# A fused RWKV, latent-attention and mixture-of-experts block: both high halves of the keys go into the stack by DMA, and the normalisations and the values' eviction go from VectorE to ScalarE

## The reference, cut to what matters

```python
x = x + rwkv(_layernorm(x))           # k, r projections; a scan over time; sigmoid(r) * y; Wo
x = x + ffn(_layernorm(x)), where ffn(x) is:
h   = _rmsnorm(x, gamma1)
q   = h @ Wq + bq                                  # [b, t, 16, 32]
k,v = split(((h @ Wdown + bdown) @ Wup + bup))     # through a latent of 64
att = softmax(einsum('bthd,btgd->bthg', q, k) / sqrt(32))   # over the 16 heads of ONE token
x   = x + (att applied to v) @ Wo + bo
h2  = _rmsnorm(x, gamma2)
out = x + sum over 8 experts of gate_e * (h2 @ We[e])       # all experts, softmax gate
```

## Time and profile before

| | us |
|---|---|
| runs | 3332.51, 3334.51, 3334.67 (median 3334.51) |
| the profiled execution, own time | 3332.17 |
| its span | 3330.30 |
| mean granted TensorE clock | 0.941 of full speed |

### The profile page before, as it was taken

The page is one execution under the profiler, slowest core; times in us unless marked ns, Lnnn a source line. Parts: engine busy times, 40 slices in busy tenths (PEclk is TensorE's granted clock), DMA queues, the critical chain, the costliest instruction groups (busy, mean ns, idle before and its releaser), DMA issues.

```text
span 3330.3 us, 53600 instructions
## 1 busy us (share of the span) xinstructions
PE 2887.2 (87%) x18864; PEld 1791.2 (54%) x18864; DVE 2476.6 (74%) x4548; ACT 956.6 (29%) x1823; POOL 686.1 (21%) x745
## 2 busy tenths in 40 slices
PE   2359999998888989989998898999889998999889
PEld 2235555554555655555564555555555555555544
DVE  5797777778777768777777777768777777877753
ACT  2243232322332322322331332232233232232320
POOL 0111222212122212222221222221222221212210
PEclk9669999999999999999999999999999999999999
DMA  6011111101111101111111111111111110111110
GB/s 192 15 24 20 33 33 26 30 24 33 20 33 27 33 20 33 20 33 26 33 27 26 20 33 30 29 26 27 27 26 33 27 33 20 32 21 33 26 20 13
DMA packets 588333, 102.96 MB, mean 31 GB/s; under 512 B 556562, under 2 KB 556690, under 8 KB 588050
## 3 DMA queue, kind: packets, MB, share of 16 engines
q1 hardware_dynamic: 588068, 99.40, 16.4%
HBM read 48.49 MB, written 16.78 MB: 20 GB/s over the span
## 4 chain that ended last, share of the span: by engine, by line
PE 62%; DVE 23%; issue 7%; SPq 5%; DMA 2%; ACT 0%; POOL 0%; DVEq 0%; ACTq 0%; POOLq 0%
PE bank L1049 49%; PE bank L1201 6%; DVE mcol L954 4%; SPq L424 4%; DVE zz L865 3%; PE bank L1079 3%; DVE ks L943 3%; DVE wkv L839 2%; PE bank L1191 2%; DMA qs<-m 2%; DVE acc L1028 1%; DVE wkv L827 1%; PE bank L1165 1%; DVE ht L935 1%; DVE zz L832 1%
## 5 line engine op out<-in xcount | busy, mean ns | idle before, releaser
L1049 PE MATMUL bank<-w_e,h2t 128*128 128x512 f16 x6144 | 1479.4, 398 | 19.1 <-DVE acc L1028 19.1
L1049 PEld LDWEIGHTS bank<-w_e,h2t 128*128 128x128 f16 x6144 | 617.9, 103 | 757.5 <-issue 123.1
L1028 DVE SCALAR_TENSOR_TENSOR acc<-bank,gates,acc 128x512 f32<-128x512 f32 x512 | 373.6, 737 | 164.7 <-PE bank L1049 163.6
L1201 PEld LDWEIGHTS bank<-vp,pr 128*128 128x128 f32 x2048 | 263.9, 197 | 24.0 <-DVE hrow L970 3.9
L1201 PE MATMUL bank<-vp,pr 128*128 128x33 f32 x2048 | 259.7, 275 | 3.8 <-ACT pr L608 2.7
L608 ACT ACTIVATE pr<-bank,col 128x512 f32<-128x512 f32 x256 | 171.9, 685 | 316.1 <-PE bank L1191 315.7
L865 DVE RECIPROCAL zz<-zz 128x256 f32<-128x256 f32 x128 | 219.1, 1733 | 46.8 <-POOL zz L462 46.8
L1049 PE MATMUL bank<-w_o,xo 128*128 128x512 f16 x768 | 174.3, 384 | 58.8 <-DVE xo L799 58.8
L455 POOL TENSOR_TENSOR e<-wkv 128x512 f32<-128x512 f32 x64 | 72.1, 1127 | 645.6 <-DVE wkv L827 645.6
L1191 PE MATMUL bank<-qs,ks 106*128 106x128 f16 x1024 | 104.5, 236 | 113.9 <-DMA qs<-m 113.9
L1182 PE MATMUL bank<-ks,qs 104*128 104x128 f16 x1024 | 90.8, 231 | 125.7 <-DMA ks<-k 65.7
(11 more groups left out here) (177 smaller groups left out, 3918.1 us busy)
## 6 DMA issues: line engine op xcount, KB each, us to landing
qs<-qo SPq DMA_DIRECT2D x384, 64.0 KB, 3.0
xk<-in_attn_x SPq DMA_DIRECT2D x32, 512.0 KB, 3.9
x<-in_attn_x SPq DMA_DIRECT2D x32, 512.0 KB, 3.6
result<-acc SPq DMA_DIRECT2D x32, 512.0 KB, 2.8
ks<-k SPq DMA_DIRECT2D x128, 64.0 KB, 3.0
w_e<-in_ffn_We SPq DMA_DIRECT2D x7, 1024.0 KB, 13.8
qs<-m SPq DMA_DIRECT2D x256, 2.0 KB, 1.7
qs<-in_attn_Wk SPq DMA_DIRECT2D x1, 1024.0 KB, 5.5
```

The costliest lines, as they stand in the source:

```text
L1028: V.scalar_tensor_tensor(out=acc[:, s, :], in0=moe_bank[u % 2][:, :], scalar=gates[:, s, e:e + 1], in1=acc[:, s, :], op0=ALU.mult, op1=ALU ...
L1049: ins = nc.tensor.matmul(dst, left(a), right(b), start=(n == 0), stop=(n == last))
L1201: ins = nc.tensor.matmul(att_bank[ATT_BANK["PV", k]][:, n * (HD + 1):(n + 1) * (HD + 1)], pr[:, k % 2, n * P:(n + 1) * P], vp[:, 4 * k + n ...
```

## The change

The first block of k high and the second are sent by SP like q's: with first = (0, 2) SP issues 8 DMAs for k high after ACT's last high half of k, and then the 4 for k low. DVE's copies and the piece att_stack are gone. ACT evicts the values. The normalisations become ACT instructions scale * x + bias, with bias = -mean * rstd, which DVE forms in one small instruction ("shift"; two in att_norm). att_norm2 is an ACT copy with a scale. att_rest moves in ORDER to behind att_vt, on ACT and on POOL.

```diff
 ORDER = [
...
-    ("moe", 1), ("att_turn", 0), ("att_rest", 0), ("mix_k", 0), ("att_latent", 0), ("att_q", 0),
-    ("att_up", 0), ("mix_v", 0), ("mix_decay", 0), ("att_stack", 0), ("moe", 2), ("mix_exp", 0),
-    ("mix_sum", 0), ("att_vt", 0), ("moe", 3), ("mix_rec", 0), ("mix_rec", 1), ("mix_scan", 0), ("moe", 4),
+    ("moe", 1), ("att_turn", 0), ("mix_k", 0), ("att_latent", 0), ("att_q", 0),
+    ("att_up", 0), ("mix_v", 0), ("mix_decay", 0), ("moe", 2), ("mix_exp", 0),
+    ("mix_sum", 0), ("att_vt", 0), ("att_rest", 0), ("moe", 3), ("mix_rec", 0), ("mix_rec", 1), ("mix_scan", 0), ("moe", 4),
...
-        stack_in = Steps(sem("stack_in"), 16, qk=16)
+        stack_in = Steps(sem("stack_in"), 16, qk=24)
...
             def att_up(t, _):
-                for src, dst, name, first in ((qo16, qs, "q", (0, 1)), (k16, ks, "k", ())):
-                    rest = 2 if first else 1
+                for src, dst, name, first in ((qo16, qs, "q", (0, 1)), (k16, ks, "k", (0, 2))):
+                    rest = 3 - sum(first)
...
+            def pre_norm(t, _):
+                act.wait_ge(*pre_dve.done(t, "shift"))
+                for s in range(SUB):
+                    nc.scalar.activation(xk_rows[:, s, :], xk_rows[:, s, :], ACT.Identity, bias=nb1[:, s:s + 1], scale=rs1[:, s:s + 1])\
+                        .then_inc(pre_act.sem, 1)
...
+            def att_norm(t, _):
+                act.wait_ge(*att_dve.done(t, "shift"))
+                if t.back(1):
+                    act.wait_ge(*att_pe.done(t.back(1), "T21"))
+                for s in range(SUB):
+                    nc.scalar.activation(h_rows[:, s, :], x1[t.par][:, s, :], ACT.Identity, bias=nb2[:, 1, s:s + 1], scale=rs2[:, 1, s:s + 1])\
+                        .then_inc(att_act.sem, 1)
+
+            def att_rest(t, _):
+                if t.back(1):
+                    act.wait_ge(*acc_pool.done(t.back(1), "acc"))
+                for s in range(SUB):
+                    nc.scalar.activation(x2[:, s, :], x1[t.par][:, s, :], ACT.Identity, bias=nb2[:, 0, s:s + 1], scale=rs2[:, 0, s:s + 1])\
+                        .then_inc(att_act.sem, 1)
...
             def att_up(t, _):
                 heads(t, "K", "k", k16, colof["kk"], bks, "k_lo", "q_lo")
+                if t.back(1):
+                    act.wait_ge(*att_dve.done(t.back(1), "ot_lo"))
+                for b in range(CB):
+                    act.wait_ge(*att_pe.done(t, f"V{b // 2}"))
+                    nc.scalar.activation(va32[:, :, b, :], att_bank[ATT_BANK["V", b // 2]][:, (b % 2) * T:(b % 2) * T + T]
+                                         .rearrange("p (g j) -> p g j", g=G), ACT.Identity, bias=bvcol[:, b:b + 1], scale=colof["vv"])\
+                        .then_inc(att_act.sem, 1)
...
+            def att_norm2(t, _):
+                act.wait_ge(*att_pool.done(t, "rms"))
+                for s in range(SUB):
+                    nc.scalar.activation(h_rows[:, s, :], x2[:, s, :], ACT.Copy, scale=rs3[:, s:s + 1]).then_inc(att_act.sem, 1)
...
             def att_norm(t, _):
-                xa = x1[t.par]
                 dve.wait_ge(*att_pool.done(t, "rstd"))
-                for s in range(SUB):
-                    V.tensor_scalar(h_rows[:, s, :], xa[:, s, :], mv2[:, s, 0:1], rs2[:, 1, s:s + 1],
-                                    ALU.subtract, ALU.mult).then_inc(att_dve.sem, 1)
...
+                for n in range(2):
+                    V.scalar_tensor_tensor(out=nb2[:, n, :], in0=mv2[:, :, 0], scalar=-1.0, in1=rs2[:, n, :], op0=ALU.mult, op1=ALU.mult)\
+                        .then_inc(att_dve.sem, 1)
...
-            def att_stack(t, _):
-
-                dve.wait_ge(*att_act.done(t, "k"))
-                for f in range(4):
-                    for n in (0, 2):
-                        V.tensor_copy(ks[n * HD:(n + 1) * HD, :, f, :],
-                                      grouped(k16, 0)[f * HD:(f + 1) * HD].rearrange("p g b j -> p g (b j)")).then_inc(att_dve.sem, 1)
...
             def att_max(t, n):
                 if n == 0:
                     pe.wait_ge(*stack_in.done(t, "qk"))
-                    pe.wait_ge(*att_dve.done(t, "stack"))
```

More of the change, by code:

```diff
@@ L280, in build @@
         wkv_pool = ("d1", 1), ("d2", 1), ("den", 1)
-        pre_dve = Steps(sem("pre_dve"), stats=2, idle=1, aggr=2, norm=2)
+        pre_dve = Steps(sem("pre_dve"), stats=2, idle=1, aggr=2, shift=1)
+        pre_act = Steps(sem("pre_act"), norm=2)
         pre_pool = Steps(sem("pre_pool"), eps=1, rstd=1)
@@ L286, in build @@
         att_pe = Steps(sem("att_pe"), **{f"{n}{k}": 1 for n, k in ATT_USES})
-        att_act = Steps(sem("att_act"), h_hi=2, c=2, q=8, k=8, ex=8, ot_hi=2, sq=2,
-                        h2_hi=2)
-        att_dve = Steps(sem("att_dve"), stats=2, idle=1, aggr=2, var=2, h=2, h_lo=2, xn=2, c_lo=1, v=4, stack=8,
-                        vt=1, smax=8, m_turn=1, m_hi=1, m_lo=1, norm=16, ot=1, ot_lo=2, x2=2, h2=2, h2_lo=2)
+        att_act = Steps(sem("att_act"), h=2, h_hi=2, c=2, q=8, k=8, v=4, xn=2, ex=8, ot_hi=2, sq=2,
+                        h2=2, h2_hi=2)
+        att_dve = Steps(sem("att_dve"), stats=2, idle=1, aggr=2, var=2, shift=2, h_lo=2, c_lo=1,
+                        vt=1, smax=8, m_turn=1, m_hi=1, m_lo=1, norm=16, ot=1, ot_lo=2, x2=2, h2_lo=2)
         gate_dve = Steps(sem("gate_dve"), gl=1, gmax=1, gsub=1, gsum=1, grec=1, gmul=1, gates=1)
         gate_act = Steps(sem("gate_act"), ge=1)
-        att_pool = Steps(sem("att_pool"), rstd=1, xb=2, q_lo=4, k_lo=4, rms=2)
+        att_pool = Steps(sem("att_pool"), rstd=1, q_lo=4, k_lo=4, xb=2, rms=2)
         acc_pool = Steps(sem("acc_pool"), acc=2)
@@ L635, in moe_gate @@
                 nc.scalar.activation(gl[:, :, :], gl[:, :, :], ACT.Exp).then_inc(gate_act.sem, 1)
-            pipeline(act, {"mix_turn": mix_turn, "mix_k": mix_k, "mix_v": mix_v, "mix_exp": mix_exp,
+            pipeline(act, {"pre_norm": pre_norm, "att_norm": att_norm, "att_rest": att_rest, "att_norm2": att_norm2, "mix_turn": mix_turn, "mix_k": mix_k, "mix_v": mix_v, "mix_exp": mix_exp,
                            "mix_num": mix_num, "mix_split": mix_split, "att_turn": att_turn,
@@ L811, in pre_norm @@
                 dve.wait_ge(*pre_pool.done(t, "rstd"))
[L812 to L814 removed]
+                V.scalar_tensor_tensor(out=nb1[:, :], in0=mv1[:, :, 0], scalar=-1.0, in1=rs1[:, :], op0=ALU.mult, op1=ALU.mult)\
+                    .then_inc(pre_dve.sem, 1)
             def mix_turn(t, _):
@@ L906, in att_norm @@
             def att_norm(t, _):
-                xa = x1[t.par]
                 dve.wait_ge(*att_pool.done(t, "rstd"))
-                for s in range(SUB):
-                    V.tensor_scalar(h_rows[:, s, :], xa[:, s, :], mv2[:, s, 0:1], rs2[:, 1, s:s + 1],
-                                    ALU.subtract, ALU.mult).then_inc(att_dve.sem, 1)
-            def att_rest(t, _):
-                xa = x1[t.par]
-                if t.back(1):
-                    dve.wait_ge(*acc_pool.done(t.back(1), "acc"))
-                for s in range(SUB):
-                    V.tensor_scalar(x2[:, s, :], xa[:, s, :], mv2[:, s, 0:1], rs2[:, 0, s:s + 1],
-                                    ALU.subtract, ALU.mult).then_inc(att_dve.sem, 1)
+                for n in range(2):
+                    V.scalar_tensor_tensor(out=nb2[:, n, :], in0=mv2[:, :, 0], scalar=-1.0, in1=rs2[:, n, :], op0=ALU.mult, op1=ALU.mult)\
+                        .then_inc(att_dve.sem, 1)
             def att_turn(t, _):
@@ L986, in att_project @@
                                            in1=x2[:, s, :], op0=ALU.mult, op1=ALU.add).then_inc(att_dve.sem, 1)
-            def att_norm2(t, _):
-                dve.wait_ge(*att_pool.done(t, "rms"))
-                for s in range(SUB):
-                    V.tensor_scalar(h_rows[:, s, :], x2[:, s, :], rs3[:, s:s + 1], None, ALU.mult).then_inc(att_dve.sem, 1)
             def att_turn2(t, _):
```

27 lines of the change are left out of this document (10 added, 17 removed).

## The result

| | us |
|---|---|
| before, 4 runs beside the changed kernel | 3330.87 to 3334.67, median 3333.51 |
| after, 4 runs | 3462.81 to 3466.43, median 3465.26 |
| ratio | 1.0395, 95% interval 1.0377 to 1.0413 |
| the profiled execution after: own time, span, mean granted clock | 3462.81, 3461.0, 0.915 |

A forecast was written before the change was run, and what follows sets the result against it. The chain from q through SP's stack DMAs, landing, scores, maxima and m was taken to bound the kernel. 30 x 5.7 = 171, iteration 32 7 and att_norm 9 gave +187 us, 3522 us against the median; range 3405 to 3590.

The forecast's parts named there:

- The chain: q ready, SP's stack DMAs, landing, scores, maxima, m, scores: moving the scores' start moves the iteration microsecond by microsecond.
- The landing, +6.1 us: SP's eight new 64 KB DMAs, 0.76 us each, delay the stack's landing by 6.1 us, between 5.4 and 8.8.
- The Trainium skill's fit: A DMA takes 2.0 us plus its bytes at 436 GB/s; by it the eight cost their issues alone, 5.4 us.
- The milder rival: q low's hold-up goes with DVE's copies, landing to scores 15.0 us: +2.3 us an iteration, 3415 us; chance 0.23.
- q low's hold-up of 1.7 us: One issue of q low's four on SP's queue was held up, 4.42 us for 2.74, possibly by DVE's copies.
- Landing to scores, 16.0 us: From stack landing to scores on PE: iteration 32's 15.36 us plus 0.67 for a lower clock; bounds 13.8 and 17.2.
- The wait for m: PE's last wait in attention, for the DMAs of m, was to stay near 4 us.
- att_norm, 9 us: Two shifts and two ACT forms of 0.75 us add 0.6 us in 15 or so iterations.
- The zeros: ACT's values, att_rest, the tail's norm2 and pre_norm cost nothing; norm2 has 0.3 us of cover before PE's need.
- "Wrong would make it": Signs against the forecast: DMA share under 0.8 with issues of 0.6 us, or PE's wait for ks under 5 us.
- The rival of no change: The eight transfers delay the landing by 2.4 us and the time stays the same; chance 0.02.

The follow-up runs named there:

- e7: The changed kernel with the stack's copies back on DVE, and mix_rec 1 and mix_scan 0 moved behind the maxima; 3288.89 us.
- e2: The kernel before with k high sent by SP's DMAs and att_stack gone, norms and values staying on DVE; 3534.58 us.
- e5: The kernel before with k high sent by SP's DMAs, plus an unused tile of 8 bytes a partition ahead of x1; 3455.38 us.
- e8: The kernel before with only an unused tile of 8 bytes a partition added ahead of x1; 3326.30 us.

## Why the prediction was right, and where it was too large

- **The chain** was read rightly: SP's queue, landing, scores, maxima, m, scores. PE's wait for the stack grew from 65.7 to 223.9 us, and the mcol waits went but for one of 0.2. That what moves the start of the scores moves the iteration microsecond by microsecond held for this change; it failed in e7, where the leg fell by 3.1 us and the iteration by 0.9, since the probabilities then waited for the recurrence.
- **The landing, +6.1 us, is the step that failed; it measured +4.15** (15.76 to 19.91). The prediction took 8 x 0.76 from the rate at full DMA engines and held everything else on the queue unchanged. The price itself was near (the issues took 0.70, and at the placement of before the engines were the limit): within one placement the eight cost 6.49 us at the old one (22.25 - 15.76, e2 against before) and 5.71 at the new one (20.04 - 14.33, e5 against e8). But the change also moves the buffers by 8 bytes, through nb1, which the prediction never looked at, and that makes all the transfers quicker: -1.43 us on the 16 old ones (e8 against before), and 5.71 - 1.43 = 4.28, against 4.15 measured. In the timeline it is q low's issues, 3.55 us for 4.42, and the last landing, 1.82 us after the last issue (1825.59 - 1823.77) for 2.73. Times 31 iterations, the step's error (6.1 - 4.15) is 60 us, the whole miss. The Trainium skill's fit that the prediction sets beside its price ("DMA: Bandwidth & Descriptors", Anatomy of one DMA) is stated there for DMAs that GpSimd issues, while SP issues these; the sum didn't use it.
- **The milder rival** was a little nearer than the forecast (3415 and 3522 around 3465), but by luck, for its cause wasn't there. It said that q low's hold-up of 1.7 us came from DVE's copies; without them, in e2, the median of the four issues stayed (4.40 for 4.41 us), and with them and the 8 bytes, in e8, it was 3.59. What came back went with the placement. That DMA issues of 64 KB at full engines pace each other was read rightly; that "full" depends on an address was not in the rows.
- **Landing to scores, 16.0 us: measured 16.11.** The lower clock behind the longer wait is the mechanism: 1.89 us for the 16 matmuls, as taken from the earlier trace rows, a granted clock of 0.50, 4.19 us for the unit. Iteration 32 took 15.75 us (15.36 before). The wait for m stayed near 4 us (3.85).
- **att_norm, 9 us: measured 12.0**, of which 4.0 in iteration 1, where before the wait was 2.6; in the other 18 times it is 8.0 us. The two ACT instructions took 0.81 us each for the 0.75 forecast.
- **The zeros** held in the steady iterations: att_rest and the values appear in no wait of PE, and DVE's low half at the tail ended 0.44 us ahead of PE's need (1878.39 + 0.75 against 1879.58; forecast 0.3). In the first iteration they did not quite hold: PE turned the rows at 148.73 for 145.77 before, with nothing there to cover the norms on ACT, +3 us; from there to the scores it gained 0.4 back.
- **The sum by measured terms**: 30 x (4.15 - 0.43) = 111.6, iteration 32 4.30 + 0.39 = 4.7, att_norm 8.0, start-up 2.6: 126.9 of the 130.7 us between the two spans; 3.8 us are not placed. The 4.15 and -0.43 are differences of medians.
- **"Wrong would make it"** named a DMA share under 0.8 with issues of 0.6 us or a wait under 5 us. The share did fall under 0.8 (0.77), but with issues of 0.70, and the wait was 6.71: half of one sign came true, and it pointed at the right place, the queue.
- **The rival of no change** put the even point at a delay of 2.4 us. That holds with the clock up (13.8 us from landing to scores); with the forecast's own 16.0 us it would be about 0.2.
